# Second norm of a transformer block one step later in the turn of attention

## The reference

```
h = patches @ W + b
x = layernorm(h)
q, k, v = heads of x @ Wq.T, x @ Wk.T, x @ Wv.T        # 12 heads of 16, q and k rotated
weights = (erf(q k^T / 4) + 1), zero above the diagonal
y = (weights @ v) / max(sum(weights), 1e-6)
h = h + y @ Wproj.T
x2 = layernorm(h)
out = h + top-2-of-8 experts(x2) (each expert takes a bounded number) + shared expert(x2)
```

## Time and profile before

| | us |
|---|---|
| median of 3 runs | 3598.76 |
| lowest, highest | 3595.02, 3599.0 |
| profiled execution, own time | 3599.66 |
| its span, first to last instruction | 3597.9 |

### The profile page before, as it was taken

How to read it: one execution, slowest core, us unless ns; L and a number is a source line. 1 busy time by engine, 2 the same in 40 slices (tenths; PEclk the granted TensorE clock), 3 DMA queues, 4 the chain that set the end, 5 groups by cost and what they waited for, 6 DMA issues and landing times. The chain is left out here.

```text
span 3597.9 us, 73107 instructions
## 1 busy us (share of the span) xinstructions
PE 3289.4 (91%) x26932; PEld 2237.2 (62%) x26932; DVE 2453.7 (68%) x4826; ACT 1595.3 (44%) x3287; POOL 1385.8 (39%) x1170
## 2 busy tenths in 40 slices
PE   6999999999999999995359999799999999999997
PEld 5677766777677777664235555566666666665665
DVE  6998999999999999996645555444444444445443
ACT  2444444444444444441024444355444444445443
POOL 1232223222222222221235552245555555555654
PEclk9899888998889889885579999999999999999999
DMA  3233233333333323331022222223323232332222
GB/s 100 70 84 71 71 71 82 84 71 64 78 82 71 75 68 82 70 57 32 33 67 70 63 74 73 80 33 62 67 37 66 36 66 39 64 64 38 43 39 30
DMA packets 330590, 227.27 MB, mean 63 GB/s; under 512 B 209103, under 2 KB 309551, under 8 KB 326159
## 3 DMA queue, kind: packets, MB, share of 16 engines
q1 hardware_dynamic: 259536, 163.94, 18.4%
q0 software_dynamic: 57472, 48.46, 9.0%
q10 hardware_dynamic: 13262, 10.65, 0.9%
HBM read 107.75 MB, written 67.85 MB: 49 GB/s over the span
## 5 line engine op out<-in xcount | busy, mean ns | idle before, releaser
L1268 DVE SCALAR_TENSOR_TENSOR ffn_hidden<-ffn_up,ffn_silu 128x490 f32<-128x490 f32 (+2 forms) x534 | 350.8, 670 | 780.1 <-ACT ffn_silu L1249 709.4
L687 POOL TENSOR_TENSOR weights<-weights,x_pair 128x400 f32<-128x400 f32 x384 | 395.1, 1029 | 865.5 <-DVE weights L559 765.8
L1249 ACT ACTIVATE ffn_silu<-ffn_gate 128x490 f32<-128x490 f32 (+2 forms) x534 | 302.1, 583 | 802.8 <-PE ffn_up L1212 778.4
L1420 POOL DMA_INDIRECT out_rows<-done,ids x256 | 409.7, 1601 | 508.3 <-ACT done L1524 429.4
L611 DVE RECIPROCAL recip<-x_product 128x200 f32<-128x200 f32 x384 | 534.4, 1392 | 0.0
L1233 PE MATMUL ffn_out<-ffn_w_hi,ffn_hidden_hi 128*126 128x192 f16 (+2 forms) x2124 | 530.2, 250 | 3.6 <-ACT done L1524 1.8
L1234 PE MATMUL ffn_out<-ffn_w_lo,ffn_hidden_hi 128*126 128x192 f16 (+2 forms) x2124 | 522.5, 246 | 0.4 <-issue 0.3
L1235 PE MATMUL ffn_out<-ffn_w_hi,ffn_hidden_lo 128*126 128x192 f16 (+2 forms) x2124 | 522.4, 246 | 0.0
L738 PE MATMUL bank<-w_qkv,normed_t 96*128 96x192 f32 (+1 forms) x1024 | 379.4, 531 | 42.6 <-ACT normed_t L409 42.6
L1261 DVE TENSOR_TENSOR ffn_hidden_lo<-ffn_hidden,ffn_hidden_hi 128x490 f16<-128x490 f32 (+2 forms) x534 | 356.4, 667 | 16.0
L1243 ACT CAST ffn_hidden_hi<-ffn_hidden 128x490 f16<-128x490 f32 (+2 forms) x534 | 320.9, 601 | 104.6 <-DVE ffn_hidden L1268 102.5
(11 more groups left out here) (180 smaller groups left out, 7300.3 us busy)
## 6 DMA issues: line engine op xcount, KB each, us to landing
patches<-in_patches SPq DMA_DIRECT2D x32, 1176.0 KB, 5.2
ffn_raw<-in_w SPq DMA_DIRECT2D x18, 768.0 KB
dram_x_t<-x_t SPq DMA_DIRECT2D x32, 392.0 KB, 3.5
x_t<-dram_x_t SPq DMA_DIRECT2D x24, 512.0 KB
base<-dram_h SPq DMA_DIRECT2D x24, 384.0 KB
out_rows<-sums ACTq DMA_DIRECT2D x24, 384.0 KB, 4.6
v_held<-v SPq DMA_DIRECT2D x64, 102.0 KB, 2.3
dram_h<-h SPq DMA_DIRECT2D x32, 192.0 KB
```

What stands on the lines that cost most here:

```text
L687: nc.gpsimd.tensor_tensor(weights[:, n % 4], weights[:, n % 4], x_pair[:, n % 4, ::-1], ALU.mult)\
L1249: nc.scalar.activation(T.silu[:, m % 2, 0:n], T.gate[m % 2][:, 0:n], ACT.Silu, scale=1.0 / (TOKEN_SCALE * WEIGHT_SCALE)).then_inc(T.silued, 1)
L1268: nc.vector.scalar_tensor_tensor(T.hidden[:, m % 2, 0:n], T.up[m % 2][:, 0:n], HIDDEN_SCALE / (TOKEN_SCALE * WEIGHT_SCALE), T.silu[:, m % ...
L1420: nc.gpsimd.indirect_dma_start(out=dram["out"][:, :], out_offset=bass.IndirectOffsetOnAxis(ap=ids[i][0:height, t, 0:1], axis=0), in_=done[ ...
```

## The change

Four parts of the work on the unit before go one step on. On VectorE the addition and spread go from step 5 to 6 and the norm from 6 to 7; on GpSimd the root goes from step 5 to 6; on TensorE the turning of x2 and on ScalarE its copies go from step 9 to 10. Within step 6 and 7 of VectorE the low halves of q and k stand ahead of them. No instruction is added or taken away, and SyncE's program is the same.

```
 ScalarE
-                    if n == 9 and has_prev:
+                    if n == 10 and has_prev:
                         act.wait_ge(x2t_out[prev], 16 * prior + 16)
                         for k, pos in enumerate(X2T):
 VectorE
-                    if n == 5 and has_prev:
+                    if n == 6 and has_prev:
                         out_of(PROJ)
                         dve.wait_ge(h_kept, u)
                         step(nc.vector.tensor_tensor(h2[prev][:], h2[prev][:], h[prev][:], ALU.add))
                         spread_of(1, h2[prev])
-                    if n == 6 and has_prev:
+                    if n == 7 and has_prev:
                         norm(1, last_root(kind, u), h2[prev], x2[prev], x2_ready)
 GpSimd
-                    if n == 5 and has_prev:
+                    if n == 6 and has_prev:
                         root(1, last_root(kind, u))
 TensorE
-                    if n == 9 and has_prev:
+                    if n == 10 and has_prev:
                         pe.wait_ge(x2_ready, 4 * u)
                         for pos, turn_part in zip(X2T, (turn_near, turn_far)):
```

## The result

The changed kernel takes 3625.51 us (median of 10 runs, 3620.14 to 3629.85) against 3598.86 for the one before (10 runs). The ratio is 1.0071, 95% interval 1.0056 to 1.0085: slower by 26 us. The profiled execution took 3624.24 us.

The account below looks back on a forecast made before the run. Attention's turn was taken as a ring through VectorE, ScalarE and TensorE. A 0.56 us delay with alternating turns gave 27.0 us, plus 0.6 each for first and last turn: +28.2 on 3599.7, median 0.9 lower, 3627 us; range 3608 to 3638.

Parts of the forecast that it names:

- The waits trade places: VectorE's step 5 wait for the projection becomes a step 6 wait for pair 7's x_pair copy, 0.50 us longer.
- The moved work behind it, 0.06 us: Step 6's two qk subtractions now precede the addition and wait for ScalarE's last cast: 0.06 us more a turn.
- 23.8 to 23.9: Sign: from step 6's x product to step 0, VectorE takes 23.8 to 23.9 us without idle.
- TensorE's wait for the floor in step 3: Sign: TensorE's wait for VectorE's floor in step 3 goes up from 0.34 to 0.9 us.
- The slacks: Copy of h has 0.4 us to spare, x2's turning in step 10 0.6; root and SyncE's transfers cost nothing.
- The clock: TensorE's low clock around the query and key block: long and short turns alternate, 53.2 and 49.2 us, averaging 51.2.
- The sum: Attention's 29 intervals give 27.0 us more, first and last turn 0.6 each: +28.2 us.
- No difference: Step 6 doesn't wait for x_pair, or TensorE's 0.34 us in step 3 absorbs it: within 7 us; chance 0.07.
- Plain delay: Attention's long turns stay 12 in 29: 17 us slower, 3616; with the smallest delay 10 us, 3609; chance 0.18.
- The faster one: TensorE's longer stand before the block makes its clock fall earlier, so long turns vanish: 3569 us; chance 0.09.

Follow-up runs that it names:

- e2: The changed kernel with TensorE's turning of x2 and ScalarE's copies put back to step 9: 3656.57 us, ratio 1.0173 to the kernel before.
- d700: The kernel before with one write of 128x700 zeros to a spare tile put before VectorE's addition: ratio 1.0095, 34 us slower.
- d1400: The kernel before with one write of 128x1400 zeros to a spare tile put before VectorE's addition: ratio 1.0148, 53 us slower.
- f8: The kernel before with eight unread 128x112 products on TensorE before the query and key block: 3521.7 us, ratio 0.9796.

## Why the prediction held

Forecast 3627, measured 3625.5. The mechanism, waits that trade places, is what the traces show. That the number is so close is in part luck: the delay was put too low and the effect of the clock too high, and the two errors nearly cancel. By its steps:

- **The waits trade places.** Right in kind and nearly to the hundredth: the x product starts 0.61 us behind the x_pair copy, which makes the stall 0.49 us longer, where 0.50 was said. The x product's waits have grown by about 74 us, where 75 was said.
- **The moved work behind it, 0.06 us.** The term was mis-sized. The casts were not waited for; the floors were not looked at, which run beside GpSimd's `cross` and take 0.66 and 0.44 us for 0.44 and 0.36, together 0.3. From the x product to the next block it is 0.28 us more than from the addition before, and to step 0 it is 24.09 us (1154.14 to 1178.23), where 23.8 to 23.9 was given as a sign. So the delay is 0.49 + 0.28 = 0.77 us a turn, not 0.56, and outside the bounds of 0.45 to 0.7. TensorE's wait for the floor in step 3 is 0.85 us in the rows above, as forecast (0.9).
- **The slacks.** In a short turn the turning of x2 in step 10 starts at 1112.46, the norm ends at 1110.71 + 1.24 = 1111.95: 0.5 us to spare (0.6 said). e2 shows what stood behind it: without the move of the turning the norm is 1.2 us late and the kernel some 35 us slower still. I had priced that only as a wait. Root, copy of h and SyncE's transfers cost nothing.
- **The clock.** The extrapolated step was the boldest. The turns alternate as forecast (49.24 and 53.16, forecast 49.2 and 53.2). But of the forecast's 27.0 us in 29 intervals, 16.2 were delay (29 x 0.56) and 10.8 the clock's; of the measured 28.0, 22.3 are delay (29 x 0.77) and 5.7 are left for the clock, whose mean from 100 to 1500 us is 0.90 in both kernels. The long turn is not longer by the whole delay, only by 0.46 (53.16 against 52.70): in the changed kernel the clock falls 0.5 us before the block starts (1130.90 and 1131.39), in the kernel before right at its start, so less of the block is slow. d700 shows that a delay alone brings the same alternation, and 31 us in the 29 intervals for a delay worth 19. What in the chip picks the kind was not settled; that it changes with the delay is shown. One reading of the earlier trace rows was wrong: TensorE waits for normed_t before the fall in the long turn only. In the short one the clock falls at 1068.5, and the wait for normed_t ends at 1071.36, behind it.
- **The sum.** 28 us forecast, 24.6 in the profiled execution, from parts that differ by more. The 29 intervals gave 28.0 (27.0 said). The first turn gave back nearly 7: from 135.49 the first addition should have gone to 135.49 + 0.50 + 3.60 (x product to addition in the rows above) = 139.6, and it stands at 132.83. That is luck and no effect of the change, for it arose ahead of the first instruction that the change moves: 1.7 us of it by 84.56 (82.87 after), the rest in that turn's block, which ran at low clock before (13.6 us at 0.50 from 112.8) and at full clock after (the low stretch is 6.8 us from 96.6, ahead of the block). The last addition of the stage, in the closing turn, whose order is unchanged, comes 21.0 us later (1688.06 against 1667.07); the remaining 3.6 us arose behind attention, where nothing was changed.
- **The rivals.** No difference is excluded by the interval. Plain delay is excluded at the price that I gave it (3609 to 3616), but with the measured 0.77 us it says 31 x 0.77 = 24 us, 3623, which lies inside the interval of 20 to 31 us. The time alone doesn't tell it from the forecast; the strict alternation of the turns does, and d700 and d1400, which cost more than their delay. The faster one, long turns vanishing, did not happen from a longer stand of TensorE; f8 shows that it happens when that stand is filled.

## What to carry to other kernels

Before moving an instruction away from a wait, look at what the next instruction on that engine waits for: here it was the very next operation of the same engine that released the first. Such a stall moves along until its own source is moved, and here the whole group had to move: less than the whole group cost 25 to 30 us, the whole group gave 49. Where an engine has two clocks, a short stand can cost twice, once itself and once in what runs slow behind it; filling it with idle products gave 73 us here. And where turns settle into a pattern, as the 102.4 us pairs here, equal times don't mean equal delays: read the delay from the rows, not from the total.

## What was not expected of the hardware

- With a stand of 1.2 us in step 9 TensorE's clock went to 1.2 GHz for 13.6 us (e2), in nearly every turn; without that stand, in the kernel before and the changed one, it did so in one turn of 29. Between the patch products that ended at 1134.5 and the fall at 1138.9 the engine had done only score and sum products and the turning.
- Time is not linear in a delay: 0.15, 0.67 and 1.40 us a turn, 5, 21 and 43 us in 31 turns, gave 3, 34 and 53 us.
- A VectorE operation of 128x264 took 0.36 us, or 0.44 or 0.66 where a GpSimd operation ran beside it for 0.15 or 0.37 us of that.
